# A six-stage decoder layer pair: where the moments of one normalisation are taken, how two stages and Mamba are written out, and the order of one transposition in the feed-forward

## The reference

```python
x = _layernorm(x + _L0_attn_ref(x, ...))        # linear attention, elu(q)+1, elu(k)+1
x = _layernorm(x + _L0_xattn_ref(x, ctx, mask)) # cross attention; it normalises x AND ctx itself first
x = _layernorm(x + _L0_ffn_ref(x, ...))         # experts choose tokens, small attention inside each
x = _layernorm(x + _L1_attn_ref(x, ...))        # Mamba: scan over 256 steps, 512 channels, 16 states
x = _layernorm(x + _L1_xattn_ref(x, ctx, ctx))  # second cross attention, no inner norm, no mask
x = _layernorm(x + _L1_ffn_ref(x, ...))         # feed-forward, activations rounded to 8-bit levels
```

```python
xn = layer_norm(x, g_x, b_x)
kvn = layer_norm(kv, g_kv, b_kv)
```

## Time and profile before

| | |
|---|---|
| median of 3 runs | 3736.04 us (3735.32 to 3744.94) |
| the profiled execution's own time | 3739.45 us |
| its span on the core | 3736.6 us |
| busy: PE / DVE / ACT / POOL | 3281.7 (88%) / 3081.5 (82%) / 2814.2 (75%) / 2522.9 (68%) us |
| mean granted TensorE clock | 0.958 of full |
| DMA, mean | 56 GB/s |
| instructions fetched by DMA | 2.47 MB and 1.38 MB |

### The profile page before, as it was taken

One profiled execution on the slowest core, in us unless ns is written; L12 is line 12 of the kernel. 1 busy time (PEld: TensorE's weight loads), 2 busy tenths in 40 slices (PEclk: granted clock), 3 DMA queues, 4 the chain that ended last, 5 costly groups with the idle time before them and its releaser, 6 DMA issues. The chain is left out here.

```text
span 3736.6 us, 75192 instructions
## 1 busy us (share of the span) xinstructions
PE 3281.7 (88%) x23360; PEld 2494.4 (67%) x23392; DVE 3081.5 (82%) x5204; ACT 2814.2 (75%) x5177; POOL 2522.9 (68%) x2900
## 2 busy tenths in 40 slices
PE   8996898879983889898989889989898879997887
PEld 5664666668472677777777777777676757775665
DVE  5665899965484899998998989999999769998887
ACT  2222777853585999898998989999899647776887
POOL 1222677740073889898888889889899836665676
PEclk9997999988997999999999999999999989998999
DMA  2111122233222111121111111111111122222111
GB/s 62 56 56 57 40 52 53 50 78 73 60 57 76 49 47 55 55 58 50 55 50 53 55 58 51 55 50 57 53 51 51 43 53 74 71 55 61 52 62 46
DMA packets 285360, 209.45 MB, mean 56 GB/s; under 512 B 131360, under 2 KB 249568, under 8 KB 285040
## 3 DMA queue, kind: packets, MB, share of 16 engines
q1 hardware_dynamic: 285040, 205.59, 20.2%
HBM read 149.05 MB, written 51.41 MB: 54 GB/s over the span
## 5 line engine op out<-in xcount | busy, mean ns | idle before, releaser
L2877 POOL TENSOR_TENSOR ma_ch<-ma_h,ma_crep 128x512 f32<-128x512 f32 x1024 | 1347.0, 1338 | 191.0 <-DVE ma_h L2988 160.3
L2988 DVE TENSOR_TENSOR_SCAN ma_h<-ma_a,ma_pbu 128x512 f32<-128x512 f32 x1024 | 1196.9, 1204 | 126.3 <-PE ma_pbu L2557 107.4
L2557 PE MATMUL ma_pbu<-ma_ident,ma_bu 128*128 128x128 f32 x4096 | 656.5, 284 | 121.4 <-DVE ma_h L2988 91.5
L2557 PEld LDWEIGHTS ma_pbu<-ma_ident,ma_bu 128*128 128x128 f32 x4096 | 482.7, 145 | 349.6 <-DVE ma_h L2988 202.4
L2766 ACT ACTIVATE ma_a<-ma_dt,ma_A 128x510 f32<-128x510 f32 x1024 | 675.6, 717 | 1.7 <-DVE ma_h L2988 1.2
L2566 PE MATMUL ma_py<-ma_ident,ma_ch 128*128 128x128 f32 x4096 | 624.0, 278 | 9.9 <-DVE ma_gT L3006 7.8
L2759 ACT ACTIVATE ma_bu<-ma_uT,ma_b_t 128x512 f32<-128x512 f32 x864 | 557.3, 716 | 12.7 <-PE ma_pbu L2557 11.0
L2566 PEld LDWEIGHTS ma_py<-ma_ident,ma_ch 128*128 128x128 f32 x4096 | 493.5, 145 | 14.4 <-DVE ma_gT L3006 11.4
L1576 POOL TENSOR_TENSOR xa_prob<-xa_e,xa_rec_head 128x616 f32<-128x616 f32 x128 | 155.7, 1217 | 126.6 <-DVE xa_rec_head L1668 114.4
L924 POOL TENSOR_TENSOR xa_prob<-xa_e,xa_rec_head 128x616 f32<-128x616 f32 x128 | 155.7, 1217 | 107.0 <-DVE xa_rec_head L1016 89.6
L362 POOL TENSOR_TENSOR la_veps<-la_mv,la_eps 128x2 f32<-128x2 f32 x32 | 6.3, 197 | 249.6 <-DVE la_mv L395 249.6
(11 more groups left out here) (376 smaller groups left out, 7863.8 us busy)
## 6 DMA issues: line engine op xcount, KB each, us to landing
ma_crep<-ma_ct_dram SPq DMA_DIRECT2D x256, 256.0 KB
xa_x<-act SPq DMA_DIRECT2D x64, 256.0 KB, 2.7
act<-xa_y SPq DMA_DIRECT2D x64, 256.0 KB, 2.2
la_x<-in_x SPq DMA_DIRECT2D x32, 256.0 KB, 2.8
act<-la_y SPq DMA_DIRECT2D x32, 256.0 KB
act<-ea_x SPq DMA_DIRECT2D x32, 256.0 KB, 4.2
ma_x<-act SPq DMA_DIRECT2D x16, 512.0 KB, 4.5
ma_xr<-act SPq DMA_DIRECT2D x16, 512.0 KB, 4.9
```

The costliest lines, as they stand in the source:

```text
L2557: last = pe.transpose(pbu[c % 2][:, t * P:(t + 1) * P], bu[:, s % 2, t, c * P:(c + 1) * P], ident[:, :])
L2877: pool.tensor_tensor(ch[:, s % 2, c], h[:, s % 2, c], crep[:, s % 4, :], ALU.mult).then_inc(multiplied, 1)
L2988: dve.tensor_tensor_scan(out=h[:, s % 2, c, :], data0=a[:, s % 2, c, :], data1=pbu[c % 2][:, :], initial=0.0, op0=ALU.mult, op1=ALU.add).t ...
```

## The change

1. The moments of the first cross attention's inner norm are taken in the linear attention. Its DVE gets `norm_moments` for the batch two back, from `la_y` while it is still in SBUF and from the context, which SP now loads there too (32 more loads); its POOL gets `norm_scale`, which writes rstd and shift of all 32 batches to tiles that outlive the stage (`Norms`). The cross attention loses `norm_stats` and `norm_scale`; ACT's `norm_apply` waits for its two loads and reads the kept tiles. The mask's two operations stay on DVE as `read_mask`, with a semaphore `mask_ready` that PE's scores, POOL's `spread_k` and SP's mask loads wait for.
2. The linear attention, the first cross attention and Mamba are written out: no hardware loop on any engine. The second cross attention and the feed-forward keep theirs.
3. In the feed-forward PE does `turn_x` ahead of `turn_h` in even slots.

```diff
+def in_order(step, turns, per, around):
+
+    for n in range(per * turns):
+        step(*(divmod(n + d, per) if 0 <= n + d < per * turns else None for d in around))
+
+class Norms:
+
+    def __init__(self, st):
+        self.rstd = st.sb("rstd", [P, B, T + 1])
+        self.shift = st.sb("shift", [P, B, T + 1])
...
             for b in range(PER):
-                store(B // PER - 1, b)
+                load_ctx(b)
+            for n in range(B):
+                store(*divmod(n, PER))
+                if n + PER < B:
+                    sp.dma_start(x[:, n % PER], batch_tiles(x_in, n + PER)).then_inc(x_loaded[n % PER], 16)
+                if 0 <= n - 1 < B - PER:
+                    sp.wait_ge(n_var, n)
+                    load_ctx(n - 1 + PER)
...
+            def norm_scale(j, b):
+                n, p = number(j, b), b % 2
+                pool.wait_ge(n_var, n + 1)
+                pool.tensor_tensor(n_neg[:, p], n_mv[:, p, :, 0], minus_one[:, :], ALU.mult)
+                link(pool.tensor_tensor(n_veps[:, p], n_mv[:, p, :, 1], eps[:, :], ALU.add))
+                link(pool.tensor_tensor(norms.rstd[:, n, :], n_veps[:, p], minus_half[:, :], ALU.pow))
+                pool.tensor_tensor(norms.shift[:, n, :], n_neg[:, p], norms.rstd[:, n, :], ALU.mult).then_inc(n_scaled, 1)
+
+            def batch(this, before, two_back):
                 if before is not None:
                     root(*before)
                 add_bias(*this)
+                if two_back is not None:
+                    norm_scale(*two_back)
...
+            def norm_moments(j, b):
+                n, p = number(j, b), b % 2
+                dve.wait_ge(y_ready, n + 1)
+                at_least(dve, n_scaled, n - 1)
+                for t in range(T):
+                    dve.bn_stats(n_stats[:, p, t, :], y[:, p, t, :])
+                dve.wait_ge(c_loaded[b], 16 * j + 16)
+                link(dve.bn_stats(n_stats[0:CTX, p, T, :], cx[:, b, :]))
+                dve.memset(spacer[:, :], 0.0)
+                for t in range(T):
+                    dve.bn_aggr(n_mv[:, p, t, :], n_stats[:, p, t, :])
+                dve.bn_aggr(n_mv[0:CTX, p, T, :], n_stats[0:CTX, p, T, :]).then_inc(n_var, 1)
...
                 dve.scalar_tensor_tensor(out=qT[:, p], in0=eq[:, p], scalar=1.0, in1=rq[:, p], op0=ALU.min, op1=ALU.add)
+                if two_back is not None:
+                    norm_moments(*two_back)
                 dve.wait_ge(kv_made, n)
...
             finish(end, PER - 2)
             residual(end, PER - 1)
+            norm_moments(end, PER - 2)
             finish(end, PER - 1)
+            norm_moments(end, PER - 1)
```

In the first cross attention (the function as a whole is moved in the file, so this is its old text against its new one):

```diff
         def batches(eng, batch, link=None):
-            in_turns(eng, batch, B // 4, 4, (0, 1, 2, -1, -2, -3), link)
+            in_order(batch, B // 4, 4, (0, 1, 2, -1, -2, -3))
...
                 if masked and n % 2 == 0:
+                    if n >= 4:
+                        sp.wait_ge(mask_ready, n // 2 - 1)
...
                 if c == 0:
+                    if masked:
+                        pe.wait_ge(mask_ready, 2 * j + b // 2 + 1)
...
             def norm_apply(j, b):
-                act.wait_ge(n_rstd_ready, number(j, b) + 1)
+                act.wait_ge(x_loaded[b], 16 * j + 16)
+                act.wait_ge(c_loaded[b], 16 * j + 16)
...
                 divide(*this, 2)
-                if after is not None and normed:
-                    norm_scale(*after)
                 divide(*this, 3)
...
                 sums(*this, 2)
-                if after is not None and normed:
-                    norm_stats(*after)
+                if after is not None and masked and after[1] % 2 == 0:
+                    read_mask(*after)
                 sums(*this, 3)
```

In Mamba `groups` becomes a plain loop of the generator; in the feed-forward:

```diff
+        def groups(group):
+            for g in range(NG):
+                group(g, g % 2, g == 0, g == NG - 1)
...
                     project(n2, 0, pgate, gate_made)
+                if not odd and n4 is not None:
+                    turn_x(n4)
                 if n is not None:
                     turn_h(n)
...
                     project(n2, 1, pup, up_made)
-                if not odd and n4 is not None:
-                    turn_x(n4)
```

More of the change, by code:

```diff
@@ L209, in linear_attention @@
         var_ready, rstd_ready, y_ready = sem("var_ready"), sem("rstd_ready"), sem("y_ready")
+        c_loaded = [sem(f"c_loaded{b}") for b in range(PER)]
+        n_var, n_scaled = sem("n_var"), sem("n_scaled")
         dve_chain, pool_chain = sem("dve_chain"), sem("pool_chain")
@@ L233, in store, with load_ctx @@
                 sp.dma_start(batch_tiles(x_out, number(j, b)), y[:, b % 2]).then_inc(y_stored[b % 2], 16)
[L235 to L238, removed]
+            def load_ctx(n):
+                sp.dma_start(cx[:, n % PER], ctx_d[n]).then_inc(c_loaded[n % PER], 16)
             for b in range(PER):
-                store(B // PER - 1, b)
+                load_ctx(b)
[6 more added lines that the diff above has]
+                    load_ctx(n - 1 + PER)
             for p in range(2):
@@ L318, in _ @@
             pe.wait_ge(w_loaded, 16 * len(loads))
[L319 removed]
+            in_order(batch, B // PER, PER, (0, 1, -1))
             last_one = (B // PER - 1, PER - 1)
@@ L349, in _ @@
             act.wait_ge(w_loaded, 16 * len(loads))
-            in_turns(act, batch, B // PER, PER, (0, 1, -1))
+            in_order(batch, B // PER, PER, (0, 1, -1))
             attended(B // PER - 1, PER - 1)
@@ L361, in root @@
                 pool.wait_ge(var_ready, number(j, b) + 1)
-                link(pool.tensor_tensor(veps[:, p], mv[:, p, :, 1], eps[:, :], ALU.add))
-                pool.tensor_tensor(rstd[:, p], veps[:, p], minus_half[:, :], ALU.pow).then_inc(rstd_ready, 1)
-            def batch(this, before):
+                link(pool.tensor_tensor(veps[:, p], mv[:, p, :, 1], eps[:, 0:T], ALU.add))
+                pool.tensor_tensor(rstd[:, p], veps[:, p], minus_half[:, 0:T], ALU.pow).then_inc(rstd_ready, 1)
+            def norm_scale(j, b):
[6 more added lines that the diff above has]
+            def batch(this, before, two_back):
                 if before is not None:
@@ L1072, in _ @@
                 dve.tensor_tensor(bo[:, :], bo[:, :], pG[0][:, D:2 * D], ALU.add).then_inc(bo_ready, 1)
-            if normed:
-                for b in range(2):
-                    norm_stats(0, b)
+            if masked:
+                read_mask(0, 0)
             unit(0, 0, 0)
@@ L2401, in tiles_until @@
             return sum(n for k, n in table.items() if k <= s)
-        def groups(eng, group, link=None, turns=NG // 2 - 1):
-            if link:
-                link.turn = None
-            group(0, 0, True, False)
-            if link:
-                link.begin(0)
-            with eng.Fori(0, turns) as j:
-                if link:
-                    link.turn = j
-                group(2 * j + 1, 1, False, False)
-                group(2 * j + 2, 0, False, False)
-            if link:
-                link.end(turns)
-            for g in range(2 * turns + 1, NG):
-                group(g, g % 2, False, g == NG - 1)
+        def groups(group):
+            for g in range(NG):
+                group(g, g % 2, g == 0, g == NG - 1)
         @block.sync
@@ L2473, in _ @@
                 load_c(0, 0, s)
-            groups(sp, group, turns=NG // 2 - 2)
+            groups(group)
             for half in range(2):
@@ L2673, in _ @@
                 turn_u(0, c)
-            groups(pe, group)
+            groups(group)
             for late in range(K - LAG, K):
@@ L2851, in _ @@
             scale_b(0, 0, 0)
-            groups(act, group, turns=NG // 2 - 2)
+            groups(group)
             for t in range(TT):
@@ L2937, in _ @@
             rms_diagonal(1)
-            groups(pool, group, link, turns=NG // 2 - 2)
+            groups(group)
             for half in range(2):
@@ L3100, in _ @@
                 step_input(0, 0, c)
-            groups(dve, group, link, turns=NG // 2 - 2)
+            groups(group)
             for t in range(TT):
```

93 lines of the change are left out of this document (40 added, 53 removed).

## The result

The changed kernel takes 3699.86 us (median of 4 runs, 3694.45 to 3701.12) where the kernel before took 3740.49 beside it (4 runs, 3735.32 to 3746.15): a ratio of 0.9888, 95% interval 0.9867 to 0.9909. It is faster by 41 us, where the sum had 70, and it lies 3 us above the top of the range. The profiled execution took 3699.94 us, with a span of 3698.2.

What follows compares the result with a forecast made beforehand. Bounds: PE in linear attention, DVE then PE in cross attention, jumps in Mamba, a three-engine cycle in feed-forward. Terms +1.5 - 28 + 0.4 - 31 - 13 = -70 us gave 3667 us, range 3646 to 3697.

Steps and rivals of the forecast that it cites:

- Mamba, -31: Mamba stage: writing out its loop saves 31 us, by removing the jumps back and the computed waits.
- with the jumps their 6 x 3.4 = 20.3 us go: Mamba: PE stands 3.4 us at each of six jumps back; written out, these 20.3 us disappear.
- I take 109.1: Mamba: a group written out takes 109.1 us, between bounds of 110.19 and 108.82, where it took 111.69.
- the first cross attention, -28: First cross attention: moving the moments out and writing out the loop saves 28 us, bounds 14 and 39.
- I take 13.0: First cross attention: a steady batch falls from 13.99 to 13.0 us, bounds 12.6 and 13.4.
- rival C: First cross attention batch stays at 13.4 us, Mamba gains its jumps alone, feed-forward nothing: 3706 us, chance 0.07.
- The 3 us for the first four batches: First cross attention: the first four batches, slow at the start for other reasons, together save 3 us.
- its cover: Linear attention: the moved moments fit DVE's idle 1.85 us before `la_kv_in`, costing a batch 0.
- B: Linear attention: the moments take 3 us, don't fit before `la_kv_in` and cost 37 us: 3704 us, chance 0.03.
- -15.3 for -13: Feed-forward: PE's new order shortens a pair of slots from 8.60 to 8.19 us, saving 13 us, bounds 0 and 19.
- D: Feed-forward: the new order is worth nothing, the rest holds: 3680 us; chance 0.24 shared with C's half measures.
- A: Written-out attention stages: fetching straight code stalls PE 3.4 us each time; with 40 stalls 3803 us, chance 0.06.

## Why the prediction was right and wrong

**Wrong: Mamba, -31 against -8 (-11 alone).** The step that failed is "with the jumps their 6 x 3.4 = 20.3 us go" together with "I take 109.1". The interval of 108.82 us came from group 14, which has no load and no squares for a group after next. The prediction named that difference and passed over it as a little work; it was the wait itself, 1.9 us in every other group. And the jumps' 20.3 us were not all on the path while that wait stood beside them: a pair lost 1.9 us by them, not 3.4. Take the wait away, and the stage gains more than the sum had: 1813.5 us, 38 less than before.

**Wrong in size: the first cross attention, -28 against -14.** DVE did stop being the bound, as said. The term "I take 13.0" was mis-sized: it measured 13.42, its own upper bound of 13.4. That bound was misread too: the 13.41 of "what the batches without loop take, moments included" is a mean of 13.4, 13.8 and 13.0, and the 13.0 is the last interval of the stage, again an odd one out; written out with their moments the steady batches took 13.6. Behind DVE I had looked at PE and at SP and had summed their work; ACT, busy 83%, held the batch by the order of its instructions in two places at once: with both changed the batch is 12.9, below the forecast. That is the half of rival C that came true ("ACT's copies and the latencies from turn to turn take the place of DVE's moments, the batch stays at 13.4"); its time, 3706, was nearer than mine, though its feed-forward was wrong. The 3 us for the first four batches did not come either.

**Right: linear attention.** The block takes 1.42 us for 1.5, and its cover holds: 0 a batch. B did not come. The stage's tail cannot be told from the 332.8 to 336.6 us that this stage took in the kernels run; from the last `la_y` to the next stage's first load it is some 4.0 us, 0.4 more than before.

**Right: feed-forward,** -15.3 for -13, and -13.9 with the order alone, so D did not come. The bound beside it was misread: DVE's own work is 150.73/20 = 7.5 us a pair in the kernel before (20 pairs), not 8.0, and what holds the fastest steady pairs at 8.00 was not looked into.

```profile
3465.00:3637.00 172.00, 153.74 (x1023) 104.94 (x1041) 150.73 (x341) 149.33 (x180) 121.32 (x341) 1.00 0.20 61
```

**Right: straight code costs nothing (against A).** PE's waits have no row in the two written-out attentions in which it stood for nothing that the profile shows, and Mamba's groups written out alone take the 110.7 that a wait for a load explains. The Trainium skill ("Runtime: NRT & Kernel Launch", "Instruction fetch mechanics") says that sequential code is fetched ahead and a taken branch off the current window stalls; this case's traces agree, with 3.3 us for each jump back in Mamba where no other wait covers it, and no such row in the straight code.

By the stage lengths of the two profiled executions, the two wrong terms make +23 and +14 against the sum and all the others together -5: 32 us of the 70 that didn't come. The last step to the predicted time has a slip of 1 us as well: 3669 less 3.4 is 3666, not 3667.

## What to carry to other kernels

- The one iteration that is faster than the others is a clue: write down what it lacks. Here the last group lacked a load, and moving four small squares by a few places was worth 30 us in the stage where writing out its loop had been worth 8 to 11.
- Gains that lie on parallel waits don't add, and may hide each other: after removing one wait, look at the next engine's order as well as its busy share, and be ready for two chains of one length, where no single edit shows anything.
- Moving work off a critical engine pays in full only if the next chain is shorter by as much; put an instruction that two others wait for earlier, where its engine already stands idle, not behind one of them.

## What the runs showed of the chip beyond that

- In Mamba of the changed kernel a load of 512 KB landed 4.9 us after its issue at the median (3.8 to 5.1), while the core moved 53 GB/s in the mean: the instruction that asked for it 3.1 us after the issue stood 1.9 us.
- A jump back over two of Mamba's groups cost PE 3.4 us in its own row, and the pair of groups 1.9 us where a load was waited for as well, 3.3 where it was not.
- Steady batches of the first cross attention mostly repeat to 0.1 us, but in six of the sixteen kernels one to three of them took 15.3 to 15.5 us where their neighbours in the pattern took 13.4 to 14.3, at places that differ between most kernels. It may be part of why the untouched stages scatter by 5.5 to 7 us; what causes it was not tried and stays open.
